# Shared expert's weights loaded at the end of attention, 23 row tiles for 24, splits and the causal product moved off GpSimd

## The reference, cut to what matters

```
xn = layernorm(x)
x = x + attn0(xn) + ffn0(xn)      # windowed attention; 64 experts, top 8, capacity 128
xn = layernorm(x)
x = x + attn1(xn) + ffn1(xn)      # below
# attn1: 16 heads of 128, tokens in blocks; silu(xn Wqkv), decay exp(-slope * distance)
#   out = (q*q_decay) kv + ((q k^T) * decay, only where key <= query) v ; rms norm ; sigmoid gate ; Wo
# ffn1: top 1 of 8 experts, hidden 512
xs = xn * sigmoid(top logit)
routed = silu(xs Wg[e]) * (xs Wu[e]) @ Wd[e]
shared = silu(xn Sg) * (xn Su) @ Sd
```

## Time and profile before

| | |
|---|---|
| median of 3 runs | 1380.31 us (1378.53 to 1382.48) |
| the profiled execution's own time | 1380.49 us |
| its span, first to last instruction | 1378.4 us |
| PE busy | 1274.4 us (92%) |
| DVE, ACT, POOL busy | 672.1, 520.5, 700.2 us |
| mean granted TensorE clock | 0.970 of full speed |

### The profile page before, as it was taken

How to read it: one execution, slowest core, us unless ns; L and a number is a source line. 1 busy time by engine, 2 the same in 40 slices (tenths; PEclk the granted TensorE clock), 3 DMA queues, 4 the chain that set the end, 5 groups by cost and what they waited for, 6 DMA issues and landing times. The chain is left out here.

```text
span 1378.4 us, 20455 instructions
## 1 busy us (share of the span) xinstructions
PE 1274.4 (92%) x7267; PEld 1028.0 (75%) x7267; DVE 672.1 (49%) x1363; ACT 520.5 (38%) x1124; POOL 700.2 (51%) x553
## 2 busy tenths in 40 slices
PE   4488899999977999999999999999999977999998
PEld 3366588888865887888788888888888863666655
DVE  4699555554577557555654335433443331222223
ACT  2344466566664433334333343333433321111110
POOL 3333487878663465677765656655565440000014
PEclk9789999999997999999999999999999997999999
DMA  6800188888652411111221111111111109311113
GB/s 225 283 1 1 45 174 182 181 182 180 126 161 82 127 59 50 58 61 54 71 76 54 51 51 61 50 51 62 50 35 35 35 0 353 116 46 47 56 50 113
DMA packets 97987, 127.38 MB, mean 92 GB/s; under 512 B 11744, under 2 KB 81248, under 8 KB 97760
## 3 DMA queue, kind: packets, MB, share of 16 engines
q1 hardware_dynamic: 82912, 99.85, 22.8%
q0 software_dynamic: 14976, 26.23, 9.5%
HBM read 97.83 MB, written 28.21 MB: 91 GB/s over the span
## 5 line engine op out<-in xcount | busy, mean ns | idle before, releaser
L1517 PE MATMUL a_p_p<-a_xr,a_wr 128*128 128x512 f32 x1152 | 308.7, 403 | 2.4 <-DVE g_x L2062 2.4
L1517 PEld LDWEIGHTS a_p_p<-a_xr,a_wr 128*128 128x128 f32 x1152 | 206.6, 189 | 42.6 <-DVE g_x L2062 3.1
L1836 POOL TENSOR_TENSOR a_sqsum<-a_sqsum,a_sq 128x512 f32<-128x512 f32 x60 | 77.9, 1298 | 228.1 <-ACT a_sq L1720 228.1
L1802 POOL TENSOR_TENSOR a_wr<-g_hold,a_wr 128x768 fp32r<-128x768 f32 x64 | 124.2, 1940 | 17.4 <-DVE a_wr L1868 17.4
L1901 DVE SCALAR_TENSOR_TENSOR a_gated<-a_th,a_p_o 128x512 f32<-128x512 f32 x64 | 44.0, 688 | 159.2 <-ACT a_sq L1720 159.2
L408 POOL DMA_INDIRECT acc<-l_ye,g_slot_token x64 | 104.8, 1637 | 32.8 <-issue 16.5
L1154 POOL DMA_DIRECT2D out<-e_ye x24 | 13.1, 547 | 193.8 <-DVE e_ye L1304 193.8
L1838 POOL TENSOR_TENSOR a_gr<-a_gated,a_gr 128x512 fp32r<-128x512 f32 x64 | 97.9, 1529 | 23.7 <-DVE a_gr L1905 23.7
L1530 PE MATMUL a_p_p<-a_wvr,a_xr 128*128 128x512 f32 x384 | 105.2, 410 | 0.3 <-DVE a_xr L1862 0.3
L1588 PE MATMUL a_p_w<-a_gr,l_wo_r 128*128 128x512 f32 x384 | 100.7, 397 | 2.3 <-POOL a_gr L1838 2.3
L1881 DVE TENSOR_TENSOR a_sc<-a_p_s,g_hold 128x512 f32<-128x512 f32 x64 | 44.1, 690 | 103.2 <-PE a_p_s L1546 102.8
(11 more groups left out here) (267 smaller groups left out, 2766.3 us busy)
## 6 DMA issues: line engine op xcount, KB each, us to landing
g_hold<-in_Wqkg SPq DMA_DIRECT2D x64, 384.0 KB, 3.2
g_hold<-in_gate_up SPq DMA_DIRECT2D x64, 192.0 KB, 3.0
g_hold<-in_Wv SPq DMA_DIRECT2D x16, 512.0 KB, 4.6
e_up<-in_gate_up SPq DMA_DIRECT2D x8, 1024.0 KB, 13.6
l_down<-in_down SPq DMA_DIRECT2D x64, 96.0 KB, 3.6
acc<-l_zero SPq DMA_DIRECT2D x2, 2176.0 KB, 11.7
l_lists<-acc SPq DMA_DIRECT2D x8, 512.0 KB, 4.9
e_down<-in_down SPq DMA_DIRECT2D x8, 512.0 KB, 12.3
```

Source lines behind the costliest of these rows:

```text
L1517: mm = pe.matmul(dst[:, :], wr[n % 2][:, wp, kk, c * P:(c + 1) * P], xr[n // H1 % 2][:, xp, kk, :], start=(kk, xp, wp) == (0, 0, 0), stop= ...
L1802: pool.tensor_tensor(wr[n % 2][:, 1, :, :], w[n % 2], wr[n % 2][:, 0, :, :], ALU.subtract).then_inc(w_parts, 1)
L1836: pool.tensor_tensor(sqsum[b % 2][:, :], sqsum[b % 2][:, :], sq[a % 2][:, :], ALU.add).then_inc(summed, 1)
```

## The change

1. `experts1` no longer loads the columns of group 0, `shared_up` and `shared_down`; SP does so at the end of `attention1`'s list, as soon as the last head has read `decay` and `qdec`, and waits for them before the barrier.
2. `RT1` is 23 for 24, one routed row tile fewer (2048 tokens in 8 experts, each rounded up to a full tile, never fill more than 23).
3. `parts(0)` and `parts(1)` are issued ahead of the 1.25 MB of layer 1's first weights.
4. GpSimd's one causal product over 128 x 2048 (L432) is gone; VectorE multiplies each head's 128 x 128 of `decay` with `causal` just before it is first used (`decay(n)`, n < 16), and waits for it.
5. The high part of the first `wv` is made by ScalarE, its low part and that of the first `w` by VectorE, in a changed order; GpSimd starts with the second of each.
6. The zeroing of `rows1` goes in pieces of 256 elements for 512.

```
-RT1 = NT + E1
+RT1 = (TOK + E1 * (P - 1)) // P
@@ layer0, sync
-            sp.wait_ge(ye_ready, E0)
+            for s in range(YR):
+                sp.wait_ge(summed[s], 16 * (E0 // YR))
+            for c in range(2):
+                parts(c)
             sp.dma_start(g["wv"], wv(io["Wv1"][0:D, :])).then_inc(next_in, 16)
             for h in range(2):
                 sp.dma_start(g["w"][h], wv(io["Wqkg1"][h * D:(h + 1) * D, :])).then_inc(next_in, 16)
-            for s in range(YR):
-                sp.wait_ge(summed[s], 16 * (E0 // YR))
-            for c in range(TPB):
+            for c in range(2, TPB):
                 parts(c)
@@ layer0, gpsimd
-            pool.wait_ge(decays_done, 1)
-            pool.tensor_tensor(g["decay"], g["decay"], causal[:, :].unsqueeze(1).to_broadcast([P, H1, P]), ALU.mult).then_inc(causal_done, 1)
@@ experts1, sync
-            tokens(0)
-            for k in range(KD):
-                sp.dma_start(shared_up[:, k, :], io["shared_up1"][k * P:(k + 1) * P, :]).then_inc(shared_in, 16)
-            sp.dma_start(shared_down, io["shared_down1"].rearrange("(k p) n -> p k n", p=P)).then_inc(shared_in, 16)
             tokens(1)
@@ experts1, tensor
-                if f == 0:
-                    pe.wait_ge(cols_in[group % 2], 16 * (group // 2 + 1))
-                    pe.wait_ge(shared_in, 48)
+                if f == 0 and group:
+                    pe.wait_ge(cols_in[group % 2], 16 * ((group + 1) // 2))
@@ attention1, sync, at the end
+            for s in range(2):
+                sp.wait_ge(cols_stored[s], 32)
+            sp.wait_ge(sc_ready, N)
+            sp.wait_ge(qd_ready, N)
+            sp.dma_start(g["cols"], g["cols1"][:, :, 0:SEQ]).then_inc(next_in, 16)
+            for kk in range(KD):
+                sp.dma_start(g["shared_up"][:, kk, :], io["shared_up1"][kk * P:(kk + 1) * P, :]).then_inc(next_in, 16)
+            sp.dma_start(g["shared_down"], io["shared_down1"].rearrange("(k p) n -> p k n", p=P)).then_inc(next_in, 16)
+            sp.wait_ge(next_in, 64)
@@ attention1, scalar, at the start
+            act.activation(wvr[0][:, 0, :, :], wv, ACT.Copy).then_inc(wv_high, 1)
             columns(0)
@@ attention1, gpsimd
-            low_v(0)
-            low_w(0)
             low_w(1)
@@ attention1, vector
             def decay(n):
+                if n < H1:
+                    dve.tensor_tensor(g["decay"][:, n, :], g["decay"][:, n, :], causal[:, :], ALU.mult).then_inc(causal_done, 1)
+                    dve.wait_ge(causal_done, n + 1)
                 dve.wait_ge(scored, n + 1)
...
-            high_v(0)
             normalise(0)
+            dve.wait_ge(wv_high, 1)
+            dve.tensor_tensor(wvr[0][:, 1, :, :], wv, wvr[0][:, 0, :, :], ALU.subtract).then_inc(wv_parts, 1)
+            low_x(0)
             last_statistics()
-            low_x(0)
             low_x(1)
+            low_x(2)
             high_w(0)
-            low_x(2)
             low_x(3)
+            dve.wait_ge(w_high, 1)
+            dve.tensor_tensor(wr[0][:, 1, :, :], w[0], wr[0][:, 0, :, :], ALU.subtract).then_inc(w_parts, 1)
             normalise(1)
```

More of the change, by code:

```diff
@@ L190, in layer0 @@
         lag = m.sb("lag", [P, P])
-        causal = m.sb("causal", [P, P])
         top8 = m.sb("top8", [P, NT, 8])
@@ L761, in decays @@
                 if i == 0:
-                    act.wait_ge(slopes_in, 80)
+                    act.wait_ge(slopes_in, 64)
                     act.wait_ge(slope_ready, 1)
@@ L1059, in _ @@
             dve.wait_ge(rstd1_ready, 1)
-            dve.wait_ge(causal_done, 1)
+            dve.wait_ge(decays_done, 1)
     return m.sems
@@ L1070, in experts1 @@
         down = m.sb("down", [P, E1, HC, D])
[L1071 to L1075, removed]
+        shared_up, shared_down = g["shared_up"], g["shared_down"]
+        cols = [g["cols"], m.sb("cols1", [P, KD, SEQ])]
         xe = [m.sb(f"xe{s}", [P, D]) for s in range(3)]
@@ L1155, in _ @@
             for s in range(2):
-                pool.wait_ge(ye_stored[s], 16 * RT1 // 2)
+                pool.wait_ge(ye_stored[s], 16 * ((RT1 + 1 - s) // 2))
             for t in range(NT):
@@ L1364, in attention1 @@
         half_norm = m.sb("half_norm", [P, H1])
+        causal = m.sb("causal", [P, P])
         xr = [m.sb(f"xr{s}", [P, 2, KD, SEQ], F32R) for s in range(2)]
@@ L1418, in attention1 @@
                  "slots_ready", "xs_ready", "c_in", "router_in", "stats_done", "var_ready", "std_ready", "rstd_ready",
-                 "xn_ready", "x_in_psum", "xT_kept", "routed", "logits_kept", "half_ready", "x_split",
+                 "xn_ready", "x_in_psum", "xT_kept", "routed", "logits_kept", "half_ready", "x_split", "next_in", "causal_done",
                  "wo_in", "wo_high", "wo_parts", "ranks_done")
@@ L1424, in attention1 @@
          chain, slots_ready, xs_ready, c_in, router_in, stats_done, var_ready, std_ready, rstd_ready,
-         xn_ready, x_in_psum, xT_kept, routed, logits_kept, half_ready, x_split,
+         xn_ready, x_in_psum, xT_kept, routed, logits_kept, half_ready, x_split, next_in, causal_done,
          wo_in, wo_high, wo_parts, ranks_done) = (m.sem(n) for n in names)
@@ L1472, in _ @@
             sp.dma_start(norm[:, :], io["norm1T"]).then_inc(c_in, 16)
+            sp.dma_start(causal[:, :], io["c_causal"]).then_inc(c_in, 16)
             output_weights(0)
@@ L2025, in _ @@
             normalise(2)
-            dve.wait_ge(c_in, 16)
+            dve.wait_ge(c_in, 32)
             dve.tensor_scalar(half_norm[:, :], norm[:, :], 0.5, None, ALU.mult).then_inc(half_ready, 1)
@@ L2092, in program @@
         g["wv"] = hold[:, V1:V1 + KD * 4 * DH1].rearrange("p (k n) -> p k n", k=KD)
+        S1, C1 = 2 * KD * F1, 2 * KD * F1 + F1 // P * D
+        g["shared_up"] = hold[:, 0:S1].rearrange("p (k n) -> p k n", k=KD)
+        g["shared_down"] = hold[:, S1:C1].rearrange("p (k n) -> p k n", k=F1 // P)
+        g["cols"] = hold[:, C1:C1 + KD * SEQ].rearrange("p (k n) -> p k n", k=KD)
         g["w"] = [hold[:, V1 + KD * 4 * DH1 + W1 * i:V1 + KD * 4 * DH1 + W1 * (i + 1)].rearrange("p (k n) -> p k n", k=KD) for i in range(2)]
```

15 lines of the change are left out of this document (7 added, 8 removed).

## The result

The changed kernel took 1363.3 us (median of four runs, 1359.37 to 1364.98), the one before 1379.88 us in the same comparison: ratio 0.9866, 95% interval 0.985 to 0.9883. Forecast were 1360.0 us and 1356 to 1364.5. So the change gains 12.8 to 16.6 us; its profiled execution, the fastest of its four, was 20.8 us shorter than the one before (last VectorE instruction 1355.4 for 1376.2 us).

A forecast was written before the change was run, and what follows sets the result against it. PE was taken to set the time nearly everywhere, so savings count only where it idles, runs slowly or loses work. 5.8 + 9.4 + 5.2 + 2.2 - 2.3 = 20.3 us off 1380.3 gave 1360.0 us, range 1356 to 1364.5.

The forecast's parts named there:

- One row tile fewer: Routed tiles of experts1: 24 become 23 on PE's chain, nothing behind moves against anything else; gain 5.8 us.
- same loss: First products behind the second barrier: slow clock costs as much as before, somewhere between none and about 3 us less.
- Shared weights ahead of the barrier: Second barrier, before experts1: loads hidden under attention1's end, so PE starts at once; gain 9.4 us.
- (b): Rival, experts1: the wait for the experts' weights replaces the shared weights' wait, up to 1.8 us, 1361.8; chance 0.05.
- (f): Rival, second barrier: the shared loads hold up the barrier, half of the 9.4 us left, 1364; chance 0.03.
- The causal product off GpSimd: End of layer0: VectorE's L985 no longer held, PE's gap shrinks and the clock stays up; gain 5.2 us.
- sums loaded first: End of layer0: GpSimd's joins come some 2 us earlier, but PE waits for none; gain 0.
- rival (a): Rival, end of layer0: the clock falls all the same, gain 2.5 us for 5.2, 1362.7; chance 0.22.
- my own sign of being wrong: End of layer0: a granted clock of 0.5 again would show the prediction wrong.
- The start of `attention1`: Start of attention1: VectorE's splits no longer held by GpSimd, first values 2.3 us earlier, 2.2 us kept.
- The causal product on VectorE: Heads of attention1: 16 small products, one blocked by GpSimd; cost 2.3 us, bounds 0.7 and 5.1.
- (c): Rival, heads of attention1: causal products blocked in more heads, cost at its upper bound, 1362.8; chance 0.09.

The follow-up runs named there:

- b_23: The kernel before with 23 row tiles and the small zeroing pieces that follow from them: 1376.66 us, ratio 0.9957 to the kernel before.
- u_shared: The changed kernel with the shared expert's loads behind the second barrier again: 1377.27 us, ratio 0.9957 to the kernel before.
- b_sums: The kernel before with the sums loaded first and nothing else: 1380.97 us, ratio 0.9984 to the kernel before.
- u_causal: The changed kernel with the causal product back on GpSimd at the end of layer0: 1364.3 us, ratio 0.9856 to the kernel before.
- again: The changed kernel unaltered, run once more, also called the repetition: 1371.64 us, ratio 0.9902 to the kernel before.
- u_start: The changed kernel with the weight splits at the start of attention1 as before: 1369.58 us, ratio 0.9893 to the kernel before.
- lag: The changed kernel without any causal product, masked distances set so large that exp gives zero: 1362.22 us, ratio 0.985 to the kernel before.
- lag_again: The kernel of lag, unaltered, run once more: 1361.31 us, ratio 0.9865 to the kernel before.
- twice: The changed kernel with each of the 16 causal products done twice: 1366.47 us, ratio 0.9902 to the kernel before.
- u_sums: The changed kernel with layer 1's weights loaded ahead of the sums again: 1364.57 us, ratio 0.9878 to the kernel before.
- fill1: The kernel of lag with useless PE products in waits at layer0's end and attention1's start and end: 1354.72 us, ratio 0.9816 to the kernel before.

## Why the prediction was right, point by point

The time came out inside the range, 3.3 us above the forecast, but not by the steps as they were written: one was explained wrongly, and others were off in ways that nearly cancel. They fared as follows.

- **One row tile fewer**, 5.8: the tile is 5.82 us, but F gave 7.7 in b_23 and 8.3 in the changed kernel, whose first eight products behind the barrier also took 5.2 us for 6.4, against the "same loss" of slow clock that I had kept. The failed half sentence on the tile is "nothing behind it moves against anything else": 1.9 us of waiting for the fetched rows went with it.
- **Shared weights ahead of the barrier**, 9.4: 8.9 by the table, 9.3 to 9.7 by u_shared; loads landed under the cover named, no wait for the experts' weights ((b) and (f) did not happen).
- **The causal product off GpSimd**, 5.2 at the end of `layer0`, and **sums loaded first**, 0: this is the step that failed. B fell by 4.6 us, but the two edits share it. Sums first alone gives 3.2 in b_sums, where the clock fell, and 5.2 in u_causal against the kernel before, where it did not; with the sums first the GpSimd product costs PE 0.2 us. I had worked out that the joins would come earlier, and then asked only who waits for the joins; the causal product behind them moved too, out of the way of the instruction that it held.
- **The clock at the end of `layer0`**: rival (a) and the forecast both happened, by execution. Of the ten profiles with either edit and without fillers, the last output product was slow in seven (changed, again, u_start, b_sums, lag, lag_again, twice) and fast in three (u_shared, u_causal, u_sums). By B the fall cost 0.5 to 3.1 us. In the changed kernel's first profile the clock fell, by my own sign of being wrong, and yet B gained 4.6 us and not (a)'s 2.5, because the clock fell only in the last tile's turn, after the values, where it had fallen ahead of them in the kernel before.
- **The start of `attention1`**, 2.2: `value(0, 0)` came 2.3 us earlier, as worked out, but C kept 1.0 (1.1 to 1.4 by u_start), since the products that start earlier run longer at the half clock: 5.49 us for 4.12.
- **The causal product on VectorE**, 2.3: 2.8 us in the first 17 heads of the first profile, with the 2.47 us block in the thirteenth head; 6.1 us in the repetition, above my upper bound of 5.1, with a granted clock of 0.97 for 0.99 there. lag's first profile lost 1.3 us in the same heads without any causal product, so not all of it is the product's. The reading "like those held up above" fits the four normalisations, which read two tensors in SBUF, and not L985, which reads one and adds a constant. That a wait puts the clock at risk was not in the sum.

Two slips of the working changed nothing: a landing 3 us behind the barrier would have cost (f) 3 us, so 1363 and not 1364, and the range does not take in every sum of two rivals, since (a) and (c) together give 1365.5.

That the sum fits is in part luck. F gave 2.5 us more than its term and A 1.0 us that belongs to none, against 0.5 less in E, 0.6 in B, 1.2 in C and 0.6 in D; so the fast profile ends 0.6 us beyond the 20.3 forecast. The median gains 16.6. Why the other three executions were 3.8 to 5.6 us slower is open: they have no profiles, and their mean granted clocks (0.979, 0.974 and, for the slowest, 0.984) don't order them against the fast one's 0.980. Of the six parts of the change one is a loss: with the sums loaded first, the causal product on VectorE costs about 2 us or more of D and saves nothing in B. The kernel with the product left on GpSimd was 7.3 us faster on the same chip, part of that by the clock. The small pieces of zeroing were never tried alone.

The Trainium skill's rule (SBUF — State Buffer, Who interferes with whom) was borne out in kind by the case it names, instructions with two inputs in SBUF: nine of the sixteen small products were held, up to 2.47 us for 0.27. The 4.35 us of L985 that the prediction puts beside it are of another form, with one input in SBUF; that instruction too was held by GpSimd's product wherever they overlapped, 4.35 us before and 2.05 in u_causal, for 0.17 when free. Whether that costs anything was decided by what else VectorE had to wait for.

## What to carry to other kernels

When a load or a step is moved earlier, follow everything that stands behind its consumer in that engine's list, not only those who wait for the consumer. Before a blocking instruction is moved to another engine, try to move it in time, or to fold it away: here a constant in a table made 16 instructions needless. On TensorE a wait cost more than its length in some executions (1.6 us more in the third head of the repetition), so a small saving in a tight loop and filler work in short gaps can be worth more than their microseconds. One profile of a kernel is not its median: compare several, cut at the same events.

## What the runs showed of the hardware

- The same wait, the same instructions, another clock: after 1.34 and 0.25 us of waiting the granted clock fell in one execution and not in the other. Much of the scatter between executions lies elsewhere, though. A ran from 383.5 to 392.3 us, and 6.4 of the 8.8 us between the first profile and the repetition had arisen by 170 us (ScalarE's first expert result at 170.54 and at 176.92). The windows from 0 to 100 and from 100 to 200 us, of the first and of the repetition:

```profile
0.00:100.00 100.00, 55.47 (x261) 44.41 (x262) 66.41 (x180) 34.85 (x102) 33.45 (x52) 0.90 0.52 173
100.00:200.00 100.00, 88.34 (x621) 71.48 (x621) 71.15 (x157) 52.44 (x142) 53.60 (x62) 0.97 0.28 64
```

```profile
0.00:100.00 100.00, 55.22 (x248) 44.00 (x251) 65.07 (x177) 34.28 (x99) 32.90 (x50) 0.98 0.52 173
100.00:200.00 100.00, 86.93 (x581) 70.65 (x589) 67.62 (x146) 49.54 (x135) 48.69 (x58) 0.93 0.23 53
```

  From 100 to 200 us the repetition has 0.04 less clock, but from 0 to 100 it has 0.08 more, where PE is busy for only 55 us. Over A as a whole the slower execution had the higher mean clock, 0.98 for 0.96. So the mean clock does not tell the time; a fall may count only where PE is waited for, and what made A longer is open.
- All profiles with the causal product on VectorE show a half clock in the last microseconds of `attention1` (from the last score product to PE's last instruction 12.9 to 13.8 us), all without it 11.8 (12.2 in fill1; the granted clock of the last 11 us is 0.80 in the changed kernel and 1.00 in lag), though that stretch holds the same instructions in both. What carries over from heads that lie 490 us back is open; no run tells.
- In fill1 the clock was full throughout a 2.93 us idle stretch and fell in the full work behind it.
